# Mixture of experts on one Trainium2 core: token weights of chunks two to four spread over the partitions by DMA, down product in plain f32

## What is computed

```python
scores = jax.nn.softmax(xf @ router_w, axis=-1)          # N x 8
topk_scores, topk_idx = jax.lax.top_k(scores, 2)
combine = zeros((N, E)).at[arange(N)[:, None], topk_idx].add(topk_scores)
g = jnp.einsum('nh,ehf->enf', xf, gate_w)                # h = f = 128
u = jnp.einsum('nh,ehf->enf', xf, up_w)
y = jnp.einsum('enf,efh->enh', silu(g) * u, down_w)
routed = jnp.einsum('enh,ne->nh', y, combine)
shared = silu(xf @ shared_gate_w) * (xf @ shared_up_w) @ shared_down_w   # 256 wide
return shared + routed
```

## Time and profile before

| | us |
|---|---|
| time, median of 3 runs (521.98 to 523.74) | 522.12 |
| the profiled execution, its own time | 523.33 |
| its span, first to last instruction | 521.3 |
| PE busy in the span | 505.4 (97%) |
| DVE, ACT, POOL busy | 425.6, 404.2, 294.5 |

### The profile page before, as it was taken

One profiled execution on the slowest core, in us unless ns is written; L12 is line 12 of the kernel. 1 busy time (PEld: TensorE's weight loads), 2 busy tenths in 40 slices (PEclk: granted clock), 3 DMA queues, 4 the chain that ended last, 5 costly groups with the idle time before them and its releaser, 6 DMA issues.

```text
span 521.3 us, 8267 instructions
## 1 busy us (share of the span) xinstructions
PE 505.4 (97%) x1993; PEld 310.4 (60%) x1993; DVE 425.6 (82%) x1631; ACT 404.2 (78%) x606; POOL 294.5 (56%) x328
## 2 busy tenths in 40 slices
PE   8789999999999999999999999999989999899997
PEld 6445555555555555555555555555555568687885
DVE  5879888988898888888888988888886667877754
ACT  3848888888888888888888888888887866657552
POOL 4435655556656566655566555666545567555652
PEclk8989999999999999999999999999999999999999
DMA  8200010001000000100010001001000000000000
GB/s 242 97 16 1 7 41 15 0 5 40 15 5 20 20 15 5 41 15 0 5 40 15 5 4 36 15 5 29 12 1 1 2 0 1 21 1 21 2 21 20
DMA packets 16070, 11.22 MB, mean 22 GB/s; under 512 B 8220, under 2 KB 13852, under 8 KB 16052
## 3 DMA queue, kind: packets, MB, share of 16 engines
q1 hardware_dynamic: 15188, 10.29, 7.1%
q10 hardware_dynamic: 864, 0.73, 0.5%
HBM read 9.96 MB, written 1.05 MB: 21 GB/s over the span
## 4 chain that ended last, share of the span: by engine, by line
PE 84%; DVE 6%; POOL 4%; issue 3%; ACT 2%; DMA 1%; DVEq 0%; POOLq 0%; ACTq 0%
PE bank L436 19%; PE bank L427 15%; PE bank L302 12%; PE bank L449 6%; PE bank L424 5%; PE bank L344 4%; PE bank L349 4%; PE bank L345 4%; PE bank L546 3%; PE bank L548 3%; PE bank L547 3%; PE bank L591 1%; PE bank L594 1%; PE bank L592 1%; PE bank L606 1%
## 5 line engine op out<-in xcount | busy, mean ns | idle before, releaser
L436 PE MATMUL bank<-hid,wf 128*128 128x512 f32 x256 | 120.2, 592 | 0.0
L917 POOL TENSOR_TENSOR rsD<-veD,c_half 128x4 f32<-128x4 f32 x32 | 37.3, 1166 | 100.7 <-DVE veD L1031 100.7
L427 PE MATMUL bank<-x,wf 128*128 128x512 f32 x192 | 93.9, 598 | 0.0
L755 ACT ACTIVATE hid<-bank,vbf 128x512 f32<-128x512 f32 x128 | 77.6, 694 | 1.9 <-PE bank L427 1.9
L436 PEld LDWEIGHTS bank<-hid,wf 128*128 128x128 f32 x256 | 46.0, 190 | 46.6 <-issue 30.8
L1002 POOL TENSOR_TENSOR xs_lo<-sc,xs_hi 128x512 fp32r<-128x512 f32 x36 | 46.6, 1296 | 41.4 <-ACT xs_hi L875 41.3
L427 PEld LDWEIGHTS bank<-x,wf 128*128 128x128 f32 x192 | 35.4, 191 | 33.7 <-issue 16.5
L1121 DVE TENSOR_SCALAR x<-bank,vln 128x256 f32<-128x256 f32 x64 | 31.9, 540 | 23.8 <-PE bank L302 23.8
L1050 DVE TENSOR_SCALAR xhB<-bank,meanB,rsB 128x128 f32<-128x128 f32 x128 | 43.8, 407 | 9.2 <-POOL rsB L917 9.2
L1050 DVE TENSOR_SCALAR xhD<-bank,meanD,rsD 128x128 f32<-128x128 f32 x128 | 43.7, 406 | 7.4 <-POOL rsD L917 3.2
L725 ACT ACTIVATE g<-bank,vbf 128x512 f32<-128x512 f32 x31 | 21.4, 691 | 35.5 <-PE bank L436 35.5
(11 more groups left out here) (173 smaller groups left out, 1178.7 us busy)
## 6 DMA issues: line engine op xcount, KB each, us to landing
wf<-in_w_f SPq DMA_DIRECT2D x16, 256.0 KB, 2.7
wu<-in_w_unit SPq DMA_DIRECT2D x10, 192.0 KB
wqkv<-in_w_qkv SPq DMA_DIRECT2D x7, 192.0 KB, 2.3
x<-in_x SPq DMA_DIRECT2D x4, 256.0 KB, 5.5
out<-ot SPq DMA_DIRECT2D x3, 256.0 KB, 2.2
wo<-in_w_o SPq DMA_DIRECT2D x8, 64.0 KB, 1.8
wmod<-in_w_mod ACTq DMA_DIRECT2D x1, 256.0 KB, 5.6
vln<-in_v_ln SPq DMA_DIRECT2D x16, 1.0 KB, 1.7
```

The lines of the kernel that those rows point to most:

```text
L427: mm = nc.tensor.matmul(ps_ff[j][:], wf1[:, j * P:(j + 1) * P], x2[(c - 2) % CH][:], start=True, stop=True)
L436: mm = nc.tensor.matmul(ps_f0[:], wf2[:, j, :], hid[:, j, :], start=(j == 0), stop=(j == FJ - 1))
L755: nc.scalar.activation(hid[:, j, :], ps_ff[j][:], ACT.Gelu_apprx_tanh, bias=vbf1[:, j:j + 1]).then_inc(h_ready, 1)
L917: nc.gpsimd.tensor_tensor(rs[buf(k, n)][:], ve[buf(k, n)][:], c_half[:], ALU.pow).then_inc(rstd_ready[k], 1)
```

## The change

- The down product of every unit is one plain f32 matmul from `wu` and `sc`. `sc_hi`, `sc_lo` and all their waits are gone; the split expert weights have only the gate and up parts (256 columns for 384).
- In chunks two to four the token weights take another way. DVE writes `cw`, a tile of 128 x 512 in which each token's 8 weights stand 16 times over. The four transposes (now at u = 0, one unit earlier) turn it into 128 partitions, of which every eighth holds one expert's weights. ACT copies all 128 partitions to `cwt`. SP then issues eight DMAs from SBUF to SBUF, one per expert, each of 128 rows of 2 KB: the 16 partitions of the expert, each repeated eight times, into a tile of its own (`spread`: `hid`, the `x2` tiles and `qk`, which the attention has finished with).
- In these chunks the `broadcast` matmul is gone. DVE multiplies silu by the spread weights (both in SBUF) as soon as silu is there, then by the up bank. Chunk one keeps the old way.
- `up(i)` now waits for the second DVE product of unit i - 2 in chunks two to four, not the first. Unit by unit the late low parts of the weights on POOL come one to two units earlier.

```diff
@@ SP
             for c in range(CH - 1):
+                sp.wait_ge(ff2_mm, NI)
+                sp.wait_ge(y2_ready, NI)
+                sp.wait_ge(cst_ready, c + 2)
+                if c:
+                    sp.wait_ge(sc_ready, E * (c + 1))
+                for e in range(E):
+                    sp.dma_start(spread[e], cwt[e::E, :].unsqueeze(1).to_broadcast([P // E, E, G])).then_inc(
+                        ld_spread[e], 16)
                 sp.wait_ge(ot_ready, c + 1)
@@ PE: up, down, the loop
-                if i >= 2:
+                if i >= 2 and i - 2 < U:
                     pe.wait_ge(su_ready, i - 1)
+                elif i >= 2:
+                    unit_done(pe, i - 2)
...
-                    k = splits(i)
-                    pe.wait_ge(sc_hi_ready, k + 1)
-                    nc.tensor.matmul(ps_y[:], wu_hi[:, u, 2, :], sc_hi[k % 2][:], start=(u == 0), stop=False)
-                    nc.tensor.matmul(ps_y[:], wu_lo[:, u, 2, :], sc_hi[k % 2][:], start=False, stop=False)
-                    pe.wait_ge(sc_lo_ready, k + 1)
-                    mm = nc.tensor.matmul(ps_y[:], wu_hi[:, u, 2, :], sc_lo[k % 2][:], start=False, stop=(u == U - 1))
+                unit_done(pe, i)
+                mm = nc.tensor.matmul(ps_y[:], wu[:, u, 2, :], sc[i % 3][:], start=(u == 0), stop=(u == U - 1))
...
-                    if i == 2 or (c and u == 1):
+                    if i == 2 or (c and u == 0):
                         weights_to_fm(c)
...
-                if u >= SHARED:
+                if c == 0 and u >= SHARED:
                     broadcast(i)
@@ POOL
-            LATE_LOW = {0: 6, 2: 7, 3: 8, 5: 9}
+            LATE_LOW = {0: 6, 1: 7, 2: 8, 3: 9}
@@ DVE: weights, products
+                if c:
+                    if c >= 2:
+                        dve.wait_ge(cst_mm, c)
+                    nc.vector.tensor_tensor(cw, comb[:].unsqueeze(2).to_broadcast([P, T, P // E, E]),
+                                            rsm[:].unsqueeze(2).unsqueeze(3).to_broadcast([P, T, P // E, E]),
+                                            ALU.mult).then_inc(cs_ready, 1)
+                    return
...
+                    dve.wait_ge(ld_spread[e], 16 * c)
+                    nc.vector.tensor_tensor(su[i % 2][:], spread[e], sg[i % 2][:], ALU.mult).then_inc(su_ready, 1)
+                    dve.wait_ge(su_ready, i + 1)
+                    dve.wait_ge(up_mm, i + 1)
+                    if i < CH * U - 1:
+                        nc.vector.tensor_tensor(sc[i % 3][:], up_bank[i % 2][:], su[i % 2][:], ALU.mult).then_inc(sc_ready, 1)
```

More of the change, by code:

```diff
@@ L101, in adaln_block @@
         cs = sb("cs", [P, T, 2, E])
-        cst = [sb(f"cst{i}", [P, G], F32R) for i in range(2)]
+        cst = sb("cst", [P, G], F32R)
+        cw, cwt = kk[:].rearrange("p (t r e) -> p t r e", t=T, e=E), kv_full
+        spread = [hid[:, j, :] for j in range(FJ)] + [x2[0][:], x2[1][:], x2[2][:], qk[:]]
         sg, su = [ek, eq], [mk, mq]
         sc = [sb(f"sc{i}", [P, G]) for i in range(3)]
-        sc_hi, sc_lo = xs_hi[2:], xs_lo[2:]
         yf = sb("yf", [P, G])
@@ L158, in adaln_block @@
         sg_ready, su_ready, sc_ready = sem("sg_ready"), sem("su_ready"), sem("sc_ready")
-        sc_hi_ready, sc_lo_ready = sem("sc_hi_ready"), sem("sc_lo_ready")
+        ld_spread = [sem(f"ld_spread{e}") for e in range(E)]
         yf_ready, out_tm, ot_ready = sem("yf_ready"), sem("out_tm"), sem("ot_ready")
@@ L201, in run @@
                 extra[place]()
-        def splits(i):
-            return min(max(i - FIRST, 0), CH * U - FIRST - 2)
         def unit_done(eng, i):
@@ L605, in broadcast @@
                 e = u - SHARED
-                nc.tensor.matmul(ps_d[:], sel[:, e * P:(e + 1) * P], cst[c % 2][:],
+                nc.tensor.matmul(ps_d[:], sel[:, e * P:(e + 1) * P], cst[:],
                                  start=True, stop=True).then_inc(bc_mm, 1)
@@ L826, in weights @@
                 act.wait_ge(cst_mm, c + 1)
-                if c >= 2:
-                    act.wait_ge(bc_mm, (c - 1) * E)
-                nc.scalar.activation(cst[c % 2][0:2 * E, :], ps_v[0:2 * E, :], ACT.Copy).then_inc(cst_ready, 1)
+                if c == 0:
+                    nc.scalar.activation(cst[0:2 * E, :], ps_v[0:2 * E, :], ACT.Copy).then_inc(cst_ready, 1)
+                else:
+                    if c >= 2:
+                        for e in range(E):
+                            act.wait_ge(ld_spread[e], 16 * (c - 1))
+                    nc.scalar.activation(cwt[:], ps_v[:], ACT.Copy).then_inc(cst_ready, 1)
             def split_h_hi(n):
@@ L839, in split_weights_hi @@
                 for u in us:
-                    nc.scalar.activation(wu_hi[:, u, :, :], wu[:, u, :, :], ACT.Copy).then_inc(wu_hi_ready, 1)
+                    nc.scalar.activation(wu_hi[:, u, 0:2, :], wu[:, u, 0:2, :], ACT.Copy).then_inc(wu_hi_ready, 1)
             def first_rows():
@@ L867, in _ @@
                     last_norm(1, NI - 2)
[L868 to L875, removed]
                 if i == U + 5:
@@ L904, in _ @@
             nc.gpsimd.memset(sel[:].bitcast(F32), 0.0).then_inc(padded, 1)
-            for i in range(2):
-                nc.gpsimd.memset(cst[i][:].bitcast(F32), 0.0).then_inc(padded, 1)
+            nc.gpsimd.memset(cst[:].bitcast(F32), 0.0).then_inc(padded, 1)
             nc.gpsimd.memset(c_half[:], -0.5).then_inc(consts_set, 1)
@@ L997, in _ @@
                         split_h(n)
[L998 to L1005, removed]
+                if i - FIRST in LATE_LOW:
+                    split_weights_lo(ORDER[LATE_LOW[i - FIRST]:LATE_LOW[i - FIRST] + 1])
         @block.vector
@@ L1198, in _, with steps @@
                   {"behind the keys": second_split})
-            STEPS = 9
+            def steps(c):
+                return 9 + 7 * (c - 1) if c else 0
             def step(n, op):
@@ L1226, in route_scores @@
             def route_scores(c):
-                n = STEPS * c
+                n = steps(c)
                 dve.wait_ge(score_mm, c + 1)
```

53 lines of the change are left out of this document (23 added, 30 removed).

## The result

| | before | changed |
|---|---|---|
| median of 5 runs each, us | 522.13 | 519.89 |
| lowest to highest, us | 521.98 to 523.74 | 519.69 to 519.99 |
| own time of the profiled execution (its span), us | 523.33 (521.3) | 519.92 (518.1) |

What follows compares the result with a forecast made beforehand. The prediction took PE, busy 97% of the span, as the bound. Waits given back -3.0, PE's work +0.3 and new waits +0.5 made -2.2 us, from 522.1 to 519.9, range 518.3 to 523.0.

Steps and rivals of the forecast that it cites:

- PE's work: On PE, 36 dearer plain down products add 5.8 us and 24 removed broadcasts save 5.5: +0.3 us.
- The rival at 0.93: Plain down product on PE costs four full steps, 0.93 us for 0.86: 2.5 us more, 522.4; chance 0.09.
- Waits given back: PE's idle spots and restarts that go with POOL's subtractions, ACT's copies and the broadcasts: 3.0 us gained.
- both of chunk one: PE's waits of 0.25 us ahead of a broadcast and 0.84 ahead of transposes in chunk one: both gone.
- the two for broadcasts: PE's waits for a broadcast's `sc`, 0.66 us in chunk two and 0.40 in chunk three: both gone, 1.06.
- the `xs` wait: PE's 1.4 us wait at 453.90 for ACT's evacuation of a bank: stays in the main, 0.25 off.
- The 0.3 at the end of the attention: POOL's shorter weight split ahead of `rsD` shortens PE's wait by way of DVE's `xhD`: 0.3 us gained.
- The new wait for `cw`: Weights wanted one unit earlier, so PE may wait at their transposes: 0.5 us for three places together.
- The balance of 9.0 against 8.9 us: Before the earlier weight transposes DVE has 9.0 us and needs 8.9: no wait, and no reserve.
- DVE the bound by POOL's reads: At chunk ends POOL's SBUF reads block DVE's `su`, with dearer `cw`: 0.8 us at three places, 522.3; chance 0.13.
- The spread: First spread tile lands 2.7 us after issue, 1.1 us in hand in chunk four: cost zero.
- The rival "slower": Spread lands late: unit 2's product, and PE, 1.7 us late in each of three chunks, 525.0; chance 0.13.

Runs made afterwards that it cites:

- plain_only: The kernel before with only the down product in plain f32, broadcasts kept, nothing of the spread: 524.88 us, ratio 1.0046 to the kernel before.
- spread_only: The changed kernel with the three-pass down product and POOL's and ACT's splits of `sc` put back: 522.94 us, ratio 1.0018 to the kernel before.
- late_transposes: The changed kernel with the token weights transposed in unit 1 of a chunk instead of unit 0: 521.08 us, ratio 0.9974 to the kernel before.
- spread_reversed: The changed kernel with its eight spreading DMAs issued from the last expert to the first: 543.23 us, a single run.

## Why the prediction was right, and where it wasn't

- **PE's work** (+5.8 - 5.5). Right, and it carried the forecast. 0.86 for the plain product came from one place of the trace; after, a unit is 2.26 long and leaves 0.86. The rival at 0.93, a chance of 0.09, is out: 36 times 0.07 would show as 2.5 us. (The Trainium skill's page "FP8 and Floating Point Precision", section TensorE Precision Notes, has four passes for true FP32; 0.93 is the estimate for them as full steps. The measurement decides, 0.86.) plain_only gives +2.7 where the terms give +5.8 less 3.0; from it to the changed kernel the spread then gives 5.0, where the terms give 5.5 less the new 0.5. Alone the halves cost +2.7 and +0.8 us, together they gain 2.2.
- **Waits given back** (3.0). Right in each size: both of chunk one, the two for broadcasts, and the `xs` wait down from 1.4 to 1.12 (from 450.02 to 451.58, less the 0.44 of four transposes), against 0.25 expected off it. The 0.3 at the end of the attention is 0.28, and the mixture gives 1.83 where the terms make 1.9. So the forecast doesn't rest on large errors that cancel; that it is met to the tenth is luck, since `cw` alone is off by 0.2. The reason given for 1.06 of it was more than was needed, though: I had these two waits go with the broadcasts, and plain_only, which keeps the broadcasts, has neither.
- **The new wait for `cw`** (0.5). 0.26, 0.04 and 0.40: 0.70 together. The sum was near, the places were not: I had most of it behind chunk one and none behind chunk three. The balance of 9.0 against 8.9 us was too close to say which.
- **DVE the bound by POOL's reads** (0.13). The mechanism is real, and the changed kernel is only just out of its reach. Two products still meet POOL's split of `h`, at the place the rival named, one in chunk two and one in chunk three; DVE, then POOL in chunk two:

```profile
454.45 1.45 DVE L1329 TENSOR_TENSOR mk<-x,ek 128x512 f32<-128x512 f32 x1 [2.36 <-ACT ek L872]
...
479.78 1.44 DVE L1329 TENSOR_TENSOR mk<-x,ek 128x512 f32<-128x512 f32 x1 [1.04 <-ACT ek L872]
```

```profile
454.07 1.27 POOL L970 TENSOR_TENSOR xs_lo<-hf,xs_hi 128x512 fp32r<-128x512 f32 x1 [6.02 <-ACT xs_hi L843]
```

  They cost DVE 0.76 and 0.75, close to the 0.8 that the rival put on each of three places. PE's waits for `cw` behind them are 0.04 and 0.40, so the first costs it next to nothing; how much of the 0.40 is the second's was not separated. What the prediction did not see is that the two halves of the change belong together for this reason: the spread alone would have met 36 reads of POOL's and gained nothing (spread_only), and the plain product is what takes them away. The prediction called the halves a cancellation on PE, which is true of PE and misses this.
- **The spread** (cost zero). Right in the result, wrong in its size. The landing of 2.7 us from loads out of HBM was too short: 3.2 to 4.3 for a first tile that somebody waited for, 4.2 and 5.0 as the page's medians for `hid` and `x`. In chunk four the first tile was thus about 0.5 ahead of silu (issue at 491.39, silu's end at 495.10), not the 1.1 of the prediction. The rival "slower" had a tile 1.7 us late in each of three chunks, and PE with it, for 525.0. late_transposes has such tiles, 2.0, 1.4 and 1.8 late, and takes 521.1, with no wait of PE for the product; spread_reversed shows the 2.4 us of slack behind silu. I had taken DVE's delay for PE's, and left out that `sc` of a unit is wanted only two units later.

## What to carry over

Before an operand of a DVE product moves from PSUM to SBUF, look at what POOL reads at that time: the cost hangs on what it meets there, and a PSUM operand (silu written back in place) is a cheap way out. A change of two halves should be costed as three: each half alone, and what each does to the engines the other leans on. A late tile is to be priced at the next reader that has no slack, not at its own.

## What the hardware showed that I had not expected

- A plain f32 matmul of 512 columns between three-pass ones takes 0.86 us, three single passes 0.70, and four full steps would be 0.93.
- Eight copies of 256 KB between SBUF and SBUF, each from 16 partitions read eight times and issued in a row on one queue, overlap, and the one issued last is there last: the first after 3.2 to 4.3 us, the last 11.8 us after the first issue, about 1.2 us for each further one.
- Beside a reading POOL instruction a DVE product with two SBUF inputs stands until POOL is done and ends 0.55 us after it; an instruction of 0.16 us took 1.25 that way.
